# Query and key rows issued by halves, one half between the maxima's store and its load

## What is computed

```python
x = x + _layernorm(_L0_attn_ref(_layernorm(x, axis=-1), ...), axis=-1)
x = x + _layernorm(_L0_ffn_ref(_layernorm(x, axis=-1), ...), axis=-1)
```

## Time and profile before

| | before |
|---|---|
| median of 3 runs | 906.02 us |
| the profiled execution: time, span | 905.31 us, 903.4 us |
| PE busy | 802.0 us, 89% of the span |
| DVE, ACT, POOL busy | 83%, 70%, 27% |
| DMA | 104.82 MB, mean 116 GB/s |
| of it SP's queue q1 | 68.31 MB, 26.9% of 16 engines |
| of it ACT's queue q10 | 31.92 MB, 9.8% of 16 engines |

### The profile page before, as it was taken

The page is one execution under the profiler, slowest core; times in us unless marked ns, Lnnn a source line. Parts: engine busy times, 40 slices in busy tenths (PEclk is TensorE's granted clock), DMA queues, the critical chain, the costliest instruction groups (busy, mean ns, idle before and its releaser), DMA issues.

```text
span 903.4 us, 24492 instructions
## 1 busy us (share of the span) xinstructions
PE 802.0 (89%) x9829; PEld 309.4 (34%) x9829; DVE 752.3 (83%) x1196; ACT 635.7 (70%) x1266; POOL 242.5 (27%) x548
## 2 busy tenths in 40 slices
PE   5279999999999999999999999999999999955950
PEld 3023334333333333343333223322332322244950
DVE  5489988999999998889999998899999999146635
ACT  6037777777776777777778989999889999931311
POOL 4110413200000415322300552441102310004773
PEclk9569999999999999999999999999999999976985
DMA  3666534665555454445313343332312131101313
GB/s 97 196 172 177 169 118 157 189 179 159 171 168 182 134 168 163 139 158 186 100 55 107 105 118 103 103 91 72 97 56 61 55 94 46 38 11 43 52 53 99
DMA packets 69478, 104.82 MB, mean 116 GB/s; under 512 B 15845, under 2 KB 45861, under 8 KB 69365
## 3 DMA queue, kind: packets, MB, share of 16 engines
q1 hardware_dynamic: 62805, 68.31, 26.9%
q10 hardware_dynamic: 5088, 31.92, 9.8%
q0 software_dynamic: 1472, 3.02, 1.6%
HBM read 84.19 MB, written 18.87 MB: 114 GB/s over the span
## 4 chain that ended last, share of the span: by engine, by line
PE 67%; DVE 9%; POOL 6%; DMA 5%; issue 4%; SPq 4%; ACT 3%; POOLq 0%; DVEq 0%
PE bank L1290 23%; PE bank L1309 20%; PE bank L1316 12%; PE bank L1270 7%; DVE unit_max L1003 4%; ACT prob_mem L901 3%; POOL prob_mem L791 3%; POOL moe_out L797 2%; DMA maxima_rows<-max_rows 2%; PE bank L1235 2%; DVE stats L946 1%; PE bank L1357 1%; PE bank L1243 1%; DMA k_parts<-prob_mem 1%; DMA bias_parts<-prob_mem 1%
## 5 line engine op out<-in xcount | busy, mean ns | idle before, releaser
L901 ACT ACTIVATE prob_mem<-bank 128x512 f32<-128x512 f32 x1024 | 556.6, 597 | 137.8 <-PE bank L1316 115.9
L1270 PE MATMUL bank<-k_rows,q_rows 56*128 56x512 bf16 x1024 | 328.2, 392 | 21.9 <-DMA k_rows<-k_parts 12.7
L1309 PE MATMUL bank<-q_rows,k_rows 59*128 59x512 bf16 x1024 | 334.3, 385 | 6.8 <-DMA q_rows<-maxima_rows 3.2
L999 DVE CUSTOM_DVE_ANT_1 no_use<-bank,w_moe 128x1024 bf16<-128x1024 f32 x256 | 305.6, 1219 | 31.0 <-PE bank L1270 28.2
L1290 PE MATMUL bank<-prob_mem,v_ring 128*32 128x256 f32 x4096 | 320.0, 386 | 7.3 <-issue 6.1
L1003 DVE TENSOR_REDUCE unit_max<-bank 128x1 f32<-128x1024 f32 x256 | 297.4, 1216 | 15.0 <-PE bank L1270 13.3
L1309 PEld LDWEIGHTS bank<-q_rows,k_rows 59*128 59x128 bf16 x1024 | 80.9, 93 | 244.5 <-ACT prob_mem L901 117.6
L702 POOL CAST max_parts<-unit_max 128x8 bf16<-128x8 f32 x64 | 12.1, 189 | 552.9 <-DVE unit_max L999 312.7
L1290 PEld LDWEIGHTS bank<-prob_mem,v_ring 128*32 128x32 f32 x4096 | 102.5, 109 | 152.8 <-ACT prob_mem L901 60.6
L1316 PE MATMUL bank<-skew_mem,pick 96*32 96x512 bf16 x1664 | 137.9, 388 | 0.0
L1270 PEld LDWEIGHTS bank<-k_rows,q_rows 56*128 56x128 bf16 x1024 | 77.0, 93 | 32.4 <-DVE unit_max L999 14.5
(11 more groups left out here) (177 smaller groups left out, 534.8 us busy)
## 6 DMA issues: line engine op xcount, KB each, us to landing
w_moe<-bias_rows ACTq DMA_DIRECT2D x31, 960.0 KB, 5.6
q_rows<-q_parts SPq DMA_DIRECT2D x252, 48.0 KB
k_rows<-k_parts SPq DMA_DIRECT2D x126, 96.0 KB
skew_mem<-bias_parts SPq DMA_DIRECT2D x32, 378.0 KB, 4.3
unit_sums<-o_ring SPq DMA_DIRECT2D x63, 128.0 KB, 2.9
w_moe<-in_L_ffn_w_dram SPq DMA_DIRECT2D x16, 256.0 KB, 3.1
q_parts<-prob_mem SPq DMA_DIRECT2D x8, 384.0 KB, 3.1
k_parts<-prob_mem SPq DMA_DIRECT2D x24, 128.0 KB, 2.7
```

Of the source, the lines that this page charges most:

```text
L901: nc.scalar.activation(prob[:, kb, half * N:(half + 1) * N], b_bank(("exp", exp_no(n, kb, half))), ACT.Exp).then_inc(exp_done, 1)
L999: nc.vector.tensor_tensor_reduce(out=no_use[:, qb % 2, :].rearrange("p (k c) -> p k c", k=QB), in0=scores.rearrange("p (k c) -> p k c", k= ...
L1270: return nc.tensor.matmul(sa_slot(QB * m + qb)[:, f, :], q_rows[rows, m % SLOTS, qb * P:(qb + 1) * P], k_rows[rows, m % SLOTS, f * N:(f + ...
L1309: return nc.tensor.matmul(b_bank(("exp", exp_no(n, kb, f))), k_rows[rows, n % SLOTS, kb * P:(kb + 1) * P], q_rows[rows, n % SLOTS, f * N:( ...
```

## The change

`maxima_of` is cut into `store_maxima` and `load_maxima`. A list `halves_to_come` holds the halves of units 4 to 63 in order, f = 1 first. `half_rows(n, many)` issues up to that many of them; it stops at a half of a unit beyond n + 4, and at unit n + 4 itself where that unit is the first of its sequence (16, 32 or 48). One half is issued between the store and the load, up to two at the old place.

```diff
-            def maxima_of(n):
+            def store_maxima(n):
 
                 slot = n % 2
                 sp.wait_ge(max_copied, n + 1)
                 sp.dma_start(maxima_dram[slot], max_rows[:, slot, :]).then_inc(mrow_stored, 16)
+
+            def load_maxima(n):
+
+                slot = n % 2
                 sp.wait_ge(mrow_stored, 16 * (n + 1))
...
+            halves_to_come = [(m, f) for m in range(LEAD, NU) for f in (1, 0)]
+
+            def half_rows(n, many):
+
+                for _ in range(many):
+                    if not halves_to_come or halves_to_come[0][0] > n + LEAD:
+                        return
+                    m, f = halves_to_come[0]
+                    if m == n + LEAD and m % H == 0:
+                        return
+                    halves_to_come.pop(0)
+                    if m >= SLOTS:
+                        sp.wait_ge(exp_done, 2 * QB * (m - SLOTS + 1))
+                    rows_of(sp, m, (f,))
...
                 if n + 1 < NU:
-                    maxima_of(n + 1)
+                    store_maxima(n + 1)
+                    half_rows(n, 1)
+                    load_maxima(n + 1)
...
-                if n + LEAD < NU:
-                    if n + LEAD >= SLOTS:
-                        sp.wait_ge(exp_done, 2 * QB * (n + LEAD - SLOTS + 1))
-                    rows_of(sp, n + LEAD)
+                half_rows(n, 2)
```

More of the change, by code:

```diff
@@ L564, in _ @@
             rows_of(sp, 2)
-            maxima_of(0)
+            store_maxima(0)
+            load_maxima(0)
             skew_of(sp, 1)
```

## The result

The changed kernel takes 910.35 us (median of 6 runs, 908.75 to 911.11); the kernel before took 906.18 us in the six runs beside it (904.73 to 907.17). The ratio is 1.0046, with a 95% interval of 1.0033 to 1.0059. That is 4.2 us or 0.46% slower, and outside the range on record.

A forecast was written before the change was run, and what follows sets the result against it. TensorE, two thirds of the chain of waits, was taken as the bound; SP's idle time costs nothing by itself. Terms 0.1 - 0.7 + 0.1 + 0.1 + 0.1 + 0.4 = +0.1 us gave 906.1 us, range 904.3 to 908.6.

The forecast's parts named there:

- Fresh rows become the wait: Rival: tops of units 14, 30 and 46 wait for late rows; +1.9 to +3.9 us, 907.9 to 909.9; chance 0.14.
- Ordinary units, nothing: Units 4 to 13, 17 to 29, 31 to 45, 47 to 63: later load costs nothing, tightest cover 0.8 us.
- Half ahead of a load, +0.2: Maxima's load: a half just ahead adds 0.2 us to its 1.8 us landing, from 0 to 1.
- Unit 2, -0.7: Iteration 1: one half less before the store, so TensorE's wait for unit 2's maxima goes, gaining 0.7 us, at least 0.5.
- Unit 14, +0.1: Iterations 12 and 13: unit 16's rows arrive 0.24 us before unit 14 starts; cost +0.1, up to 0.6 or 1.3.
- With iteration 12 free of rows I take that case: Unit 14: the store lands within 2.5 us, as in unit 15 (2.04), not in the old 4.10.
- Unit 30, +0.1: Iterations 28 and 29: unit 32's rows ready 6.73 us after the store, against 6.97 available; +0.1, ends as at unit 14.
- Unit 46, +0.4: Iterations 44 and 45: unit 48's rows replace the maxima as the wait, start 613.8 not 613.41; +0.4, from -0.1 to +1.2.
- Slow issues, +0.1: Ordinary units: an issue about 1 us slow between store and load eats the cover and 0.2 to 0.4 more; +0.1.
- three margins of 0.24, 0.24 and -1.4 us: Units 14, 30 and 46: time to spare before TensorE needs the fresh rows; unit 46 was to stand about 1.4 us.

The follow-up runs named there:

- the first experiment: The change, but rows of units 16, 32 and 48 issued at their old place, half in the gap kept: 910.45 us, ratio 1.0051 to before.
- the split version: The change, but a fresh unit's first half goes in its own iteration, only its second in the next gap: 905.98 us, ratio 0.9997 to before.

## Why the prediction was wrong

It gave 906.1 us, from 904.3 to 908.6, and 0.22 to slower. What came is the rival *Fresh rows become the wait*, given 0.14 and 907.9 to 909.9, at exactly its three places, with the clock's fall on top in some executions; 910.35 lies 0.45 above its upper end. Two steps failed. The terms for units 14 and 30, +0.1 each, rested on a store that lands within 2.5 us and on issues of their usual length; they measured 1.1 to 1.4 and 0.5 to 1.2. And the sum had no term for the clock, which cost another 1.2 behind unit 46's wait in the profiled execution. The steps in turn:

- **Ordinary units, nothing: right.** In stage 1 the load mostly goes 2.6 us behind the store where 2.52 was worked out, and TensorE starts 1.9 us or more behind it. From unit 3 on no ordinary unit of the two profiles stands for its maxima but unit 48, behind a slow issue.
- **Half ahead of a load, +0.2: a little too much.** From load to TensorE, with a half ending 0.04 us earlier: 613.88 to 615.63, 1.75 us, in the first experiment; 612.07 to 613.93, 1.86 us, in the split version; 1.76 us without one. At unit 1, where TensorE waited for them, it was 2.1 to 2.3 us in the profiles, against 1.82 and 1.70 in the two of before. The price is 0 to 0.1 in the main part and 0.3 to 0.6 at unit 1. The Trainium skill, in "DMA: Bandwidth & Descriptors", section "Queues, rings and completion order", lets a load's increment come only behind every earlier write of its DMA engines, so a backlog would be paid in full. The trace doesn't contradict it. The engines' busy tenths in 611.6 to 615.6 us of the first experiment, 40 slices of 0.1 us:

```profile
DMA  3899630000432695385000001497930000100166
```

  The half's last DMA is issued at 613.36, the load at 613.88. The block from 614.0 to 614.6 is the half's last data, and the load's own few packets come from 614.8, 0.9 us after its issue, as early as the prediction gave them without a half. So the half is just out of the way.
- **Unit 2, -0.7: wrong.** The wait for the maxima went in the profile of after (in the second one 0.29 us of it stayed, since the load went 5.57 us behind the store), and unit 2 started 0.8 us closer to before than unit 1. But unit 2 then took 13.04 us instead of 12.27, and by unit 4 all was given back. Inside unit 2, VectorE worked without a break:

```profile
84.08 1.21 DVE L1018 CUSTOM_DVE_ANT_1 no_use<-bank,w_moe 128x1024 bf16<-128x1024 f32 x1
...
85.61 0.68 DVE L1029 TENSOR_TENSOR bank<-bank,w_moe 128x512 f32<-128x512 f32 x1
```

The same instruction in the kernel before stands 1.11 us earlier, as much as unit 1 started earlier there:

```profile
84.50 0.68 DVE L1010 TENSOR_TENSOR bank<-bank,w_moe 128x512 f32<-128x512 f32 x1
```

In the changed kernel ACT and then TensorE waited for that last one:

```profile
86.33 0.60 ACT L920 ACTIVATE prob_mem<-bank 128x512 f32<-128x512 f32 x1 [0.85 <-DVE bank L1029]
```

```profile
87.28 0.64 PE L1309 MATMUL bank<-prob_mem,v_ring 128*32 128x256 f32 x8 [0.78 <-issue]
```

  The step that failed is "So the stall goes: -0.7": the stall did go, but TensorE wasn't what set the pace of that unit, VectorE was. In the first experiment unit 2 did the same, starting 0.65 us closer and giving it back.
- **Unit 14, +0.1: 1.1 to 1.4.** The sum had 6.73 us from the store to the rows' arrival against 6.97 of cover. It was 8.37 us (230.51 to 238.88). The store to the load took 3.76 instead of 2.52, the rest of SP's way 2.32 instead of 2.26, and the landing 2.29 instead of 1.95. The failed premise is "With iteration 12 free of rows I take that case", the fast landing of iteration 15: the skew was 4.5 us ahead as forecast, and the load was late all the same. The half itself, 3.13 us instead of 2.15, would have put the load about 3.5 us behind the store, but the store was no faster. The version without a half in the gap shows it alone, with the same skew, store and load in iteration 13:

```profile
226.41 0.56 SPq L440 DMA_DIRECT2D skew_mem<-bias_parts  x1
...
230.90 0.29 SPq L501 DMA_DIRECT2D maxima_rows<-max_rows  x1
234.52 0.55 SPq L509 DMA_DIRECT2D q_rows<-maxima_rows  x2
```

  The skew is 4.49 us ahead, no rows were issued in iteration 12, nothing lies between store and load, and still they are 3.62 us apart. In the version with a fresh unit's halves split, the skew is 4.50 ahead and the load 3.91 behind the store, though the half takes only 2.42. So the distance to the skew, on which the premise rested, doesn't set the landing by itself; what does was not found. In all three profiled kernels that have the change's order in iteration 13 (the change, and the two with units 16 and 32 alone put off), the load goes 3.5 to 3.8 us after the store.
- **Unit 30, +0.1: 0.5 to 1.2.** 8.20 us instead of 6.73 from store to TensorE, by the same split: 1.07 more to the load, 0.10 on SP, 0.30 in the landing. The cause of the first is a slow issue, 1.66 us instead of 0.70. I had priced slow issues only where they delay the maxima in ordinary units, not where two of them stand in a chain with 0.24 us to spare.
- **Unit 46, +0.4: right in mechanism, +0.65.** 7.01 us from store to TensorE (610.48 to 617.49), where 6.73 was worked out; 0.12 each in the load and on SP, and 0.04 in the landing of 1.99. The releaser that the profile names is "issue", not the rows, but the last row DMA lies 1.99 us ahead, near the 2.29 and 2.25 of the other two places.
- **The clock: missing from the sum.** 1.2 us in the profiled execution of after, 1.2 to 1.4 in four of the experiments (the first, units 16 and 32 alone, no half in the gap, no half in 29 and 45). It follows the wait, so it made a wait of 1.7 us cost 2.9.
- **Slow issues, +0.1: 0.1 to 0.6.** Unit 48 stood 0.55 us, because the pair at 632.26 took 2.13 us instead of 0.70 in the gap of its own maxima.

The median's 4.2 us is then 2.2 to 3.3 us of waits for rows (the sum over the three units in the two profiles), and the rest the clock in some executions and slow issues; this last split was not measured apart. The chance of 0.14 was too low above all because three margins of 0.24, 0.24 and -1.4 us were each set against single durations, the same ones three times over. In the profiled execution the clock and unit 48's wait, neither of which the rival held, make 1.8 of the 5.8 us.

## What to carry to other kernels

Idle time on an issuing queue is worth nothing until someone waits for what it issues; when it is filled, ask what is pushed behind the filler and when its consumer needs it. Here all fresh rows had to be issued ahead of the maxima's load, and one half on each side of the maxima's store restored the time (905.98 us). Both behind the store cost about 3 to 4 us; both ahead of it cost 0.16% at the top of the next iteration and 0.51% at the old place with another half in the gap, where the store came late. A margin on a chain of ten issues and two landings has to cover one slow issue (0.5 to 1.4 us here) and the scatter of a landing (2.1, 3.8 and 4.0 us for unit 29's store in three profiles with the same order), and a wait of TensorE should be priced at more than its length.

## What the hardware showed that I had not expected

**Slow issues come with instruction packets.** In the two profiles of the change and the first of before, 50 of SP's issues between 50 and 800 us took over 0.5 us more than the median of their line and shape. At 46 of them a packet of the queue q8, which the profile calls "instruction", begins within 0.7 us of the issue's start, though there is only one such packet in 10.5 us, so that about 7 would be expected by chance. The queue's row in the DMA view of 439 to 442 us (packets, MB, share of 16 engines):

```profile
q8 instruction: 1, 0.02, 2.6%
```

It falls beside the pair of issues at 439.67, which took 1.66 us instead of 0.70. Such issues lie at nearly the same places of SP's program in both profiles of the change (142, 189, 209, 361, 517, 561 and 655 us in the first), but their size varies: the pair that took 1.66 us at 439.67 took 1.04 in the second profile, where unit 30 loses 0.5 us instead of 1.2. That the fetch causes the delay is a reading of this coincidence; no run took it away.

**The clock fell after some waits and not after others of like length.** After waits of 1.68 and 1.74 us it fell to 1.2 GHz for 3.4 us; after 1.62 and 1.68 us, at the same unit of the same or nearly the same kernel, it did not, and neither did it after 2.64 us in the version without a half in the gap:

```profile
615.20 0.37 PE L1328 MATMUL bank<-q_rows,k_rows 59*128 59x512 bf16 x1 [1.68 <-issue]
```

```profile
625.19 0.37 PE L1327 MATMUL bank<-q_rows,k_rows 59*128 59x512 bf16 x1 [2.64 <-issue]
```

The first is unit 46 of the split version with unit 48 put off, the second unit 46 of the version without a half in the gap; the granted clock stays at 1.0 behind both. How often it falls in executions that were not profiled is open. A hint is each execution's mean granted clock, 0.947 in the profile with the fall and 0.949 in the one without: of the change's first six executions three have 0.947 (910.23 to 911.11 us), two 0.948 and one 0.949 (908.75 us, the fastest).

**The start-up scatters.** Unit 1 starts at 69.00 and 69.73 us in two profiles of the same kernel before, and at 70.12 and 69.25 in two of the change. Later in stage 0 a single landing can scatter as much: unit 29's store, with the same order around it, was followed by its load after 2.11 us in the first experiment, 4.00 with unit 48 alone put off, and 3.78 without the half in the gaps of iterations 29 and 45.
